# Four chained attention layers: layer 1's sums from keys folded on POOL, gelu in two halves, several steps moved in the written order

## The reference

```
kv = concat([ctx, latents]) @ kv_w + kv_b
attn = softmax(where(mask, (latents @ q_w + q_b) . kmat / DH, -inf))
out = rmsnorm((attn . v) @ out_w + out_b + latents)
out = gelu(out @ mlp_w1 + mlp_b1) @ mlp_w2 + mlp_b2 + latents        # tanh gelu, 512 -> 2048 -> 512
```

## Time and profile before

| | |
|---|---|
| median of 3 runs | 3415.44 us (3411.43 to 3416.31) |
| the profiled execution | 3403.19 us, its span 3401.4 us |
| mean granted TensorE clock | 0.921 of full speed |
| PE busy | 2862.4 us (84%), 15392 matmuls |
| DVE busy | 1857.7 us (55%) |
| ACT busy | 1330.2 us (39%) |
| POOL busy | 647.2 us (19%) |

### The profile page before, as it was taken

The page is one execution under the profiler, slowest core; times in us unless marked ns, Lnnn a source line. Parts: engine busy times, 40 slices in busy tenths (PEclk is TensorE's granted clock), DMA queues, the critical chain, the costliest instruction groups (busy, mean ns, idle before and its releaser), DMA issues. The chain is left out here.

```text
span 3401.4 us, 42637 instructions
## 1 busy us (share of the span) xinstructions
PE 2862.4 (84%) x15392; PEld 1333.0 (39%) x15392; DVE 1857.7 (55%) x4546; ACT 1330.2 (39%) x2320; POOL 647.2 (19%) x594
## 2 busy tenths in 40 slices
PE   4888888877999999998889898986657888888895
PEld 1222222224555555555555455542222333333332
DVE  3777777723333333311445555656777866667641
ACT  0555555542333333322333333232214544554562
POOL 1566666651000000000000000001110101000000
PEclk7999999988999999999999999997778999999997
DMA  4444444221001101112223223233243223223210
GB/s 96 99 96 97 97 96 97 68 95 35 8 27 54 56 29 33 63 44 75 48 47 70 61 46 65 57 68 76 59 101 82 70 57 85 70 68 75 59 38 19
DMA packets 182339, 220.00 MB, mean 65 GB/s; under 512 B 40841, under 2 KB 135665, under 8 KB 175985
## 3 DMA queue, kind: packets, MB, share of 16 engines
q1 hardware_dynamic: 170064, 189.74, 24.2%
q0 software_dynamic: 6016, 20.98, 1.8%
q10 hardware_dynamic: 6048, 6.56, 0.6%
HBM read 146.90 MB, written 51.64 MB: 58 GB/s over the span
## 5 line engine op out<-in xcount | busy, mean ns | idle before, releaser
L1248 DVE TENSOR_REDUCE l_M<-PS 128x1 f32<-128x512 f32 x512 | 329.0, 680 | 169.1 <-PE PS L720 168.7
L1474 DVE TENSOR_REDUCE l_M<-PS 128x1 f32<-128x512 f32 x512 | 334.5, 682 | 138.7 <-PE PS L960 135.6
L1187 ACT ACTIVATE l_P<-PS 128x512 f32<-128x512 f32 x512 | 286.5, 598 | 252.8 <-PE PS L970 234.5
L1547 POOL TENSOR_TENSOR l_S<-l_P 128x512 f32<-128x512 f32 x256 | 326.4, 1307 | 56.6 <-ACT l_P L1043 56.6
L1043 ACT ACTIVATE l_P<-PS 128x512 f32<-128x512 f32 x512 | 276.3, 599 | 138.2 <-PE PS L729 134.7
L1313 DVE TENSOR_REDUCE l1a_M<-PS 128x1 f32<-128x512 f32 x256 | 158.9, 682 | 254.3 <-PE PS L782 254.3
L960 PE MATMUL PS<-l_KS,l_QS 97*128 97x512 bf16 x512 | 205.0, 411 | 101.5 <-DVE l_M L1474 70.3
L720 PE MATMUL PS<-l_KS,l_QS 97*128 97x512 bf16 x512 | 205.1, 411 | 79.4 <-DVE l_M L1248 40.7
L1380 DVE CUSTOM_DVE_ANT_0 l_JK<-PS,l_MK 128x256 f32<-128x256 f32 x512 | 195.7, 419 | 124.2 <-PE PS L890 121.5
L855 PE MATMUL PS<-l_w_mlp_w,l_H 128*128 128x512 f32 x512 | 240.2, 615 | 14.2 <-ACT l_H L1130 7.2
L1152 ACT ACTIVATE l_P<-l_P 128x1024 f32<-128x1024 f32 x128 | 134.6, 1056 | 273.6 <-DVE l_P L1394 272.4
(11 more groups left out here) (242 smaller groups left out, 4605.0 us busy)
## 6 DMA issues: line engine op xcount, KB each, us to landing
l_QS<-q_scratch SPq DMA_DIRECT2D x128, 128.0 KB, 5.6
q_scratch<-l_T SPq DMA_DIRECT2D x96, 128.0 KB
l_QS<-q_scratch SPq DMA_DIRECT2D x32, 384.0 KB, 4.8
k_scratch<-l_T SPq DMA_DIRECT2D x96, 128.0 KB
l_KS<-k_scratch SPq DMA_DIRECT2D x32, 384.0 KB
l_QS<-q_scratch SPq DMA_DIRECT2D x32, 256.0 KB, 5.6
l_KS<-k_scratch SPq DMA_DIRECT2D x32, 256.0 KB
l_RB<-l_recs SPq DMA_DIRECT2D x32, 256.0 KB
```

The source lines that it names most:

```text
L1187: e.activation(t.P[quad % 4][:, m, :], PS[:, COUNTS.bank[st], :], ACT.Exp, scale=0.25).then_inc(q.sem("act.exp", st), 1)
L1248: e.tensor_reduce(t.M[i % 2][:, qt, hd:hd + 1], PS[:, COUNTS.bank[st], :], AX.X, ALU.max).then_inc(q.sem("dve.smax", st), 1)
L1474: e.tensor_reduce(t.M[i % 2][:, qt, hd:hd + 1], PS[:, COUNTS.bank[st], :], AX.X, ALU.max).then_inc(q.sem("dve.smax", st), 1)
L1547: x = e.tensor_tensor(t.S[j % 2][:, m, :], t.P[2 * j % 4][:, m, :], t.P[(2 * j + 1) % 4][:, m, :], ALU.add)
```

## The change

- Layer 1's sums: a new step "1.fold" on POOL, four an item, adds the two key blocks of a score step's weights, P[:, :, 0:256] + P[:, :, 256:512]; the second and fourth also add their result to the one before. So all 512 keys of a head are folded on 128 partitions in S. A new step "1.sums", two an item, makes four products with ones over S in a bank of ring A, and ACT copies that. "1.vals" keeps only the products with V. ACT's exp now also waits for the fold of the item before.
- Score products: both K.Q products of a step first, then both of the mask.
- The two "1.vals" of one score step stand side by side in the order; the first "1.sums" right behind the last, the second after the next item's smax and a projection. fetch, inv, spread, f0, f1 and the root's steps are later by 0.06 to 0.15 of an item.
- "2.gelu" is two instructions of half the columns at 0.8 and 0.9 (it was one at 0.93); "2.fc2" parts 0 and 1 wait only for the first half, and fc2 starts at 1.16, not 1.11. "2.kproj", "2.ksplit" and "2.v" go from 3.36, 3.38, 3.42 to 2.95, 3.0, 3.03.
- Layer 0: "0.sums" goes from 0.8625 to 0.9251 + n/4, which is right behind "0.vals" on PE; "0.sout", "0.fetch", "0.inv", "0.spread" follow.

```diff
@@ layer0_order
-            out += [(0.51 + n / 4, k("fold", n)), (0.8625 + n / 4, k("sums", n))]
+            out += [(0.51 + n / 4, k("fold", n)), (0.9251 + n / 4, k("sums", n))]
         for g in range(2):
-            out += [(0.8 + g / 2 + 0.01, k("out", g)), (1.1125 + g / 2 + 0.01, k("sout", g))]
+            out += [(0.8 + g / 2 + 0.01, k("out", g)), (1.175 + g / 2 + 0.01, k("sout", g))]
...
-        out = [(0.8, k("fetch")), (0.98, k("inv")), (0.99, k("spread"))]
+        out = [(0.84, k("fetch")), (0.99, k("inv")), (1.0, k("spread"))]
@@ layer1_order
-        out += [(2.28 + 0.2 * n + 0.05 * m, k("vals", 2 * n + m)) for n in range(4) for m in range(2)]
-        out += [(2.55, k("out", 0)), (2.95, k("out", 1)), (3.05, k("fetch")), (3.15, k("inv")), (3.2, k("spread"))]
+        out += [(2.31 + 0.2 * n + 0.0001 * m, k("vals", 2 * n + m)) for n in range(4) for m in range(2)]
+        out += [(2.3 + 0.2 * n, k("fold", n)) for n in range(4)]
+        out += [(2.9102 + 0.2098 * n, k("sums", n)) for n in range(2)]
+        out += [(2.55, k("out", 0)), (2.95, k("out", 1)), (3.2, k("fetch")), (3.3, k("inv")), (3.35, k("spread"))]
         if h:
-            out += [(3.35, k("f0")), (3.47, k("f1", 0)), (3.54, k("f1", 1)), (3.6, k("f1b")), (3.7, k("guess"))]
-            out += [(3.72 + 0.02 * n, k("newton", n)) for n in range(3)] + [(3.8, k("f2"))]
+            out += [(3.48, k("f0")), (3.58, k("f1", 0)), (3.65, k("f1", 1)), (3.7, k("f1b")), (3.78, k("guess"))]
+            out += [(3.79 + 0.02 * n, k("newton", n)) for n in range(3)] + [(3.86, k("f2"))]
@@ layer2_order
-            out += [(0.11 + 0.1 * j, k("fc1", j)) for j in range(8)] + [(0.93, k("gelu")), (0.9, k("lload"))]
-            out += [(1.11 + 0.1 * j + 0.05 * (j // 4), k("fc2", j)) for j in range(8)]
+            out += [(0.11 + 0.1 * j, k("fc1", j)) for j in range(8)] + [(0.8, k("gelu", 0)), (0.9, k("gelu", 1)), (0.9, k("lload"))]
+            out += [(1.16 + 0.1 * j + 0.02 * (j // 4), k("fc2", j)) for j in range(8)]
...
-            out += [(3.36, k("kproj")), (3.38, k("ksplit")), (3.42, k("v")), (3.62, k("mkload")), (3.75, k("mk")),
+            out += [(2.95, k("kproj")), (3.0, k("ksplit")), (3.03, k("v")), (3.62, k("mkload")), (3.75, k("mk")),
@@ tensor1
-                for k in range(2):
-                    ks = slice((2 * half + k) * 128, (2 * half + k) * 128 + 128)
+                keys = [slice((2 * half + k) * 128, (2 * half + k) * 128 + 128) for k in range(2)]
+                for k, ks in enumerate(keys):
                     for m in range(4):
...
-                                 t.Q[i % 3][32 * m:32 * m + 32, g, :], start=True, stop=False, tile_position=(32 * m, 0),
+                                 t.Q[i % 3][32 * m:32 * m + 32, g, :], start=(k == 0), stop=False, tile_position=(32 * m, 0),
                                  skip_group_check=True)
+                for k, ks in enumerate(keys):
                     for m in range(4):
...
-                for m in range(4):
-                    x = e.matmul(PS[32 * m:32 * m + 32, 6, 256:512], ones[:, :], P[:, m, cut],
...
+            elif kind == "1.sums":
+                q.wait_ge("pool.fold", step("1.fold", i, 2 * j + 1))
+                bank = q.bank_empty(st)
+                for m in range(4):
+                    x = e.matmul(PS[32 * m:32 * m + 32, bank, 0:256], ones[:, :], t.S[j][:, m, :], start=True, stop=True,
+                                 tile_position=(0, 32 * m), skip_group_check=True)
+                x.then_inc(q.sem("pe.sums", st), 1)
@@ scalar1, scalar2
             elif kind == "1.sc":
                 q.wait_ge("pe.vals", step("1.vals", i - 1, 2 * j + 1))
+                q.wait_ge("pool.fold", step("1.fold", i - 1, j))
...
             elif kind == "2.gelu":
-                q.wait_ge("act.fc1", step("2.fc1", 2 * b, 7))
-                e.activation(t.H1[:, :, :], t.H1[:, :, :], ACT.Gelu_apprx_tanh).then_inc(q.sem("act.gelu", st), 1)
+                x = t.H1[:, 8 * j:8 * j + 8, :]
+                q.wait_ge("act.fc1", step("2.fc1", 2 * b, 4 * j + 3))
+                e.activation(x, x, ACT.Gelu_apprx_tanh).then_inc(q.sem("act.gelu", st), 1)
@@ gpsimd1
+            elif kind == "1.fold":
+                g, half = divmod(j, 2)
+                q.wait_ge("pe.sums", step("1.sums", i - 1, g))
+                q.wait_ge("act.exp", step("1.sc", i, j))
+                to = t.S2 if half else t.S[g]
+                if half:
+                    q.wait_ge("pool.fold", step("1.fold", i, 1) if g else step("1.fold", i - 1, 3))
+                x = e.tensor_tensor(to[:, :, :], t.P[j][:, :, 0:256], t.P[j][:, :, 256:512], ALU.add)
+                x.then_inc(q.sem("pool.fold", st), 1)
+                if half:
+                    q.wait_ge("pool.fold", st, less=1)
+                    e.tensor_tensor(t.S[g][:, :, :], t.S[g][:, :, :], t.S2[:, :, :], ALU.add).then_inc(q.sem("pool.fold", st), 1)
```

More of the change, by code:

```diff
@@ L251 @@
     "1.v": ["pe.v", "dve.v"], "1.smax": ["pe.smax"] + 4 * ["dve.smax"], "1.rows": ["dve.rows"], "1.turn": ["pe.turn", "act.turn"],
-    "1.sc": ["pe.sc"] + 4 * ["act.exp"], "1.vals": ["pe.vals"], "1.out": ["act.sums", "act.vals"], "1.inv": ["dve.inv"],
+    "1.sc": ["pe.sc"] + 4 * ["act.exp"], "1.vals": ["pe.vals"], "1.fold": ["pool.fold"], "1.fold1": ["pool.fold"], "1.fold3": ["pool.fold"], "1.sums": ["pe.sums", "act.sums"], "1.out": ["act.vals"], "1.inv": ["dve.inv"],
     "1.f0": ["pool.f0"], "1.f1": ["pe.f1", "dve.f1", "dve.f1b"], "1.f1b": ["act.f1"], "1.newton2": ["dve.newton"],
@@ L848, in tensor2 @@
                 tt, part = divmod(j, 4)
-                q.wait_ge("act.gelu", step("2.gelu", 2 * b))
+                q.wait_ge("act.gelu", step("2.gelu", 2 * b, part // 2))
                 q.wait_ge("w2m", ("2.start1", 0, 0, 0))
@@ L1094, in scalar1 @@
                 q.wait_ge("pe.vals", step("1.vals", i, 4 * j + 3))
-                q.wait_ge("put", step("1.out", i, 0) if j else step("1.out", i - 1, 1))
-                e.activation(t.SS[:, :], PS[:, 6, 256:512], ACT.Copy).then_inc(q.sem("act.sums", st), 1)
                 q.wait_ge("pe.f1", step("1.f1", 2 * b - 3, 1))
@@ L1099, in scalar1 @@
                 e.activation(t.AT[b % 2][:, 2 * h + j, :], PS[:, 6, 0:256], ACT.Copy).then_inc(q.sem("act.vals", st), 1)
+            elif kind == "1.sums":
+                q.wait_ge("put", step("1.sums", i, 0) if j else step("1.sums", i - 1, 1))
+                q.wait_ge("pe.sums", st)
+                e.activation(t.SS[:, :], PS[:, COUNTS.bank[st], 0:256], ACT.Copy).then_inc(q.sem("act.sums", st), 1)
             elif kind == "1.f1b":
@@ L1637, in sync_sums @@
             if kind == y + "fetch":
-                q.wait_ge("put", step(y + ("sout" if y == "0." else "out"), i, 1))
+                q.wait_ge("put", step(y + ({"0.": "sout", "1.": "sums"}.get(y, "out")), i, 1))
                 q.wait_ge("rec", step(y + "inv", i - 2))
@@ L1715, in sync1 @@
                     e.dma_start(t.KX[b % 2][32 * m:32 * m + 1, :], t.MB[b % 2][0:1, :]).then_inc(q.sem("mrow", st), 16)
-            elif kind == "1.out":
+            elif kind == "1.sums":
                 q.wait_ge("spread", step("1.spread", i - 4))
@@ L1757, in sync2 @@
                 q.wait_ge("pe.vals", ("1.vals", B - 1, 1, 3))
+                q.wait_ge("pool.fold", ("1.fold", B - 1, 1, 1))
                 e.dma_start(t.X[b % 4][:, :, :], tokens(x1[b])).then_inc(q.sem("inl", st), 16)
```

9 lines of the change are left out of this document (4 added, 5 removed), and 6 rows, old and new, of tables (FILLS, LATER, MOVES).

## The result

The changed kernel takes 3315.4 us (median of 4 runs, 3310.6 to 3330.6), the kernel before 3414.8 in the same comparison: a ratio of 0.972, 95% interval 0.969 to 0.975, some 96 us faster. The forecast was 3310. The profiled execution is the slowest of the four, 3330.6 us with a span of 3328.8, and that of before is faster than its own median; so the spans of the two traces differ by 72.6 us only.

What follows compares the result with a forecast made beforehand. PE was taken to bound layer 1, mostly PE with waits layer 2, no engine alone layer 0. Terms -45 - 50 - 10 = -105 us took the profiled 3403.2 to 3298, with a 12 us offset 3310 us; range 3268 to 3365.

Steps and rivals of the forecast that it cites:

- Layer 1, -45: Layer 1: fewer sums products on PE save 2.8 us an item over 16 items, 45 us; bounds 41 and 52.
- the 0 for the grouping: Layer 1's score step: grouping K-products and mask-products gains nothing; bounds 0 and 6 us of gain.
- The turn's 6 us: Layer 1's turn: PE's 0.89 us wait for the row maxima's parts in every second item goes, 6 us gained.
- POOL's 8: Layer 1: the store of y delays the fourth fold, so PE waits 1.2 us at second sums sets, 8 us lost.
- Layer 2, -50: Layer 2: both gelu halves ahead of the first exp save 7.7 us an element, some 50 us; bounds 0 and 82.
- Less 2 for the new wait: Layer 2: 2 us an element lost to a new wait and to the place that k and v left.
- Layer 0, -10: Layer 0: sums next to values save 15 us of PE, two thirds taken, 10 us; bounds -20 and +5.
- The wait only moves: Layer 2: DVE's k split holds up adds and smaxes, PE waits there; gain 15 not 50, 3345 us; chance 0.17.
- Everything hits: Layer 2 at 11 us an element and layer 0 at 15: 3280 us; chance 0.10.
- POOL holds DVE up: Layer 1: POOL's adds lengthen DVE's two-input row-maxima steps, costing 53 us: 3363 us; chance 0.08 (mild).
- Slower than before: Layer 1: the same POOL and DVE contention at full size, ten meetings a pair cost 168 us: 3478; chance 0.03.
- The change does not do what it says: Layer 1: folds come too late and PE waits on POOL at each sums set; priced at 1.2 us, no chance given.

Runs made afterwards that it cites:

- e4: The changed kernel with layer 1's K-products and mask-products alternating again, 4 and 4, instead of 8 and then 8: 3320.7 us, ratio 0.972.
- e11: The changed kernel with layer 2's q projections and their splits 0.08 earlier: 3333.9 us, ratio 0.977.
- e1: The kernel before with layer 1's part of the change alone, layers 0 and 2 as before: 3373.9 us, ratio 0.989.
- e10: The changed kernel with layer 2's output products (the two f1 steps) one or two smax steps later: 3286.0 us, ratio 0.963.
- e2: The kernel before with layer 2's part of the change alone: 3353.1 us, ratio 0.984.
- e7: The kernel before with only layer 2's k projection, its split and v moved up, the gelu whole in its old place: 3390.4 us, ratio 0.994.
- e6: The kernel before with layer 2's part, but k projection, its split and v in their old place: 3382.1 us, ratio 0.991.
- e3: The kernel before with layer 0's part of the change alone: 3405.1 us, ratio 0.999.
- e5: The kernel before with layer 2's part, but the gelu as one instruction ahead of the first exp: 3365.9 us, ratio 0.986.
- e12: The changed kernel with the root's last step ahead of layer 1's last V copy and layer 2's output products later: 3280.0 us, ratio 0.961.
- e8: The changed kernel with the store of y on POOL put behind the next item's fourth fold: 3320.9 us, ratio 0.973.

## Why the prediction was right, and where it was not

The forecast of 3310 against 3315 is right in sign and size. The main terms came from the right places, but that the sum is only 5 us off is in part luck: layers 1 and 0 gave 6 each less than forecast, layer 2 gave 5 more, and inside layer 2 the terms were off both ways.

**Layer 1, -45, measured -39 (33 to 44).** The removed sums, 2.8 us an item, were right: a pair should fall by 5.6, gain 0.89 at the turn and lose 1.33 on POOL, 5.16 in all; it fell by 5.27. The wait on POOL was forecast at 1.2 with its place and cause. The columns' price held, and so did the 0 for the grouping (e4). Two slips are in the text itself. The turn's 6 us against POOL's 8 are a loss of 2, which "-45" leaves out; and by its own terms a pair comes to 84.3 - 5.6 - 0.9 + 1.2 = 79.0 us, not to the 78.5 named as the sign.

What failed is that the last item was priced like the others. It was to gain 2.8 us. In the five traces with the change's order of layer 1 it takes 44.5 to 44.6 us four times and 41.9 once (e11), mean 44.0; in the six with the old order 41.6 to 45.6, mean 43.4. So it gained nothing, and that is about 3 of the 6 us that are missing. Two things come together there: the wait of 2.07 us that the change brought, since no projection is left to cover the folds, and a lower clock behind it, which is not the change's own. The 32 us show 0.58 in the changed kernel, e1, e4 and e10, 0.75 in e11 with the same order; and with the old order, where PE waits 0.95 us for the maxima and 0.69 for an exp, 0.89 in the kernel before, 0.84 in e2 and e7, 0.85 in e6 and 0.74 in e3 and e5. Whether the longer wait is what makes the clock stay low longer is likely by these rows, and not shown: no run removes this wait. The other 3 us are within the interval.

**Layer 2, -50, measured -55 (47 to 63).** The mechanism was right in its main term: the wait at the values went, 5.3 us an element over the four even ones (forecast 5.5). The second term, 2.4 us for the lower clock behind it, did not come in the sum: PE's busy time over four elements is the same before and after (411.3 and 411.4 us), so what the products behind this wait gained was lost behind others. Per element the forecast was 7.7 and the trace has 6.5, all of it idle time. Of the terms, the waits for DVE's adds and the turn's transfer went wholly in 1600 to 2200 us, 9.9 + 8.4 us in five elements (3.7 each, where I took 1.8). Two that I had left out went too, the one for ACT's copies of y and nearly all of the one for the split q on its way back from scratch (0.8 us in three are left). They are these in the kernel before:

```profile
PE PS L901 <- DMA l_QS<-l_MT: 9.9, 5, 3.1
PE PS L890 <- DMA l_QS<-q_scratch: 9.4, 6, 3.8
PE PS L901 <- DVE l_P L1394: 8.4, 10, 1.5
PE PS L890 <- ACT l_YT L1115: 6.5, 5, 1.3
```

So 5.3 + 3.7 + 1.3 + 1.1 (the split q; the one of 3.8 lies ahead of these elements) = 11.4 us of waits are gone; against it stand 2.2 for POOL, 2.3 for the gap without a releaser and 1.1 for the copy of k, 5.6: together 5.8, and the rest of the 6.5 is in waits under 0.5 us. If the gap without a releaser is a transfer of the split q, as e11 suggests, this last wait has not gone but moved to the element's other item, and grown. "Less 2 for the new wait" named ACT's copies and the smaxes; the copy was 1.1, and I had missed the other two. The one for POOL comes so: in the kernel before, the output products start 4.4 to 6.2 us after POOL's multiplication ends (three elements of 1870 to 2120 us), and between the wait at the values and them stands a part of fc2 (L855, 4.9 us from 1882.66). The change removes that wait and, with fc2 at 1.16, puts this part behind the output product (at 1943.94, the product being at 1938.27); only k projection and v, 3.7 us, come in. So the chain of sums, four transfers and that multiplication has less time than it takes; I had looked at that chain in layer 1 only. It is this stretch that counts and not the element's length: e11, with 114.1 us, waits for POOL, and e7, with 115.0, doesn't. The first elements gave more than the 5 us I put there: the one ahead of these four lasts 94.8 us (1564.43 to 1659.19), before 108.2 (1600.27 to 1708.47). With it the traces put some 43 us of gain between layer 1's last turn and the last element's start (47 in e2); the rest of the 55 is not located.

**Layer 0, -10, measured -4 (-10 to +1).** The term is mis-sized: of 15 us of PE work I took two thirds, and a quarter is what came. A possible reason shows in the trace of the changed kernel. PE's waits for DVE's maxima in 200 to 640 us, changed kernel:

```profile
PE PS L722 <- DVE l_M L1259: 26.5, 23, 3.8
PE PS L612 <- DVE l_M L1259: 24.0, 12, 3.3
```

50.5 us, and 42.2 in the kernel before (30.5 at the smaxes, 11.7 at the projections): 8 us more, as if so much of the saved work had become waiting for DVE, as the sentence "a shorter way to such a wait is only a longer wait" has it. But in e3 the two are 44.2 us, 2 more than before, and the layer's length scatters by 16 us between traces of one order. That DVE takes the gain is a guess from these rows, which e3 speaks against; that there is a gain is not shown either.

**The rivals.** *The wait only moves* is false for the change and true in the main for one edit of it (e7, 0.9 us an element). *Everything hits* did not come, but 3280 is what e12 reaches. *POOL holds DVE up* did not happen: the root's steps L643 and the maxima's L1332 stay at their 0.15 and 0.19 us in layer 1, for the reason given, that they fall where POOL is idle; e8 shows the mechanism at full size, once a fold may start earlier, and shows that it is this order that avoids it. I had counted the two-input steps alone; a one-input step (L645) is held as well. *Slower than before* would have needed six or seven such meetings a pair on PE's path; e8 has two, and its pair grew by 1.2 us although a wait of 1.33 had gone. *The change does not do what it says* is false: only every fourth sums set waits, 1.33 us.

Of what the text said would show it: the pair came at 79.07 (78.5), PE at 98%, no wait at the turn, an element at 109.4 (107 to 109), no wait over 3 us at the values; but the clock in layer 2 stayed at 0.94 over the whole window (0.97 to 2078 us), not 0.98, and layer 0's 10 us did not show.

## What to carry to other kernels

When a wait on one engine is removed from a repeating chain, list every other chain with a fixed latency that runs over the same stretch (sums, transfers, reciprocals, back to an operand): the removed wait was time that they had too, and the longest of them becomes the next wait. Moving its consumer a step later can be worth more than the wait itself, since the products behind the wait ran at the lower clock as well (e10). Price the last item of a pipeline by itself, since the work that covers a chain in the others is missing there. A queue entry that looks as if it blocks the next one (a store in front of an add) may be what keeps two engines apart; before moving it, look at what the other engine does in the time in which the add would then run (e8). A shortened burst on an engine that waits for another anyway is worth a fraction of its length (15 us of work in layer 0, 4 measured, and even these not clear of noise). And before a stretch of two traces is compared, look at the same stretch in every other trace of the same order: the last item of layer 1 varies by 4 us among kernels that don't differ in it.
